# A fused two-layer transformer kernel in f32: the layer norm moves from VectorE to ScalarE, several steps move by a slot or two, and in even slots the gated products run between the two bias steps

## The reference

```
xn = layernorm(x)
x  = x + attn0(xn) + ffn0(xn)      # 16 heads, rope, window bias, causal softmax,
                                   # relu(probs + tau/row), Wo; FP4-quantised silu-gated FFN, I = 352
xn = layernorm(x)
x  = x + attn1(xn) + moe1(xn)      # linear attention: elu(q)+1, elu(k)+1, running state;
                                   # 4 experts (top 2) and a shared one, I = 344
layernorm(x) = (x - mean) / sqrt(var + 1e-5)
```

## Time and profile before

| what | value |
|---|---|
| median of three runs | 2307.14 us |
| profiled execution | 2310.34 us |
| its span on the core | 2308.5 us |
| mean granted TensorE clock | 0.971 of full speed |
| busy: TensorE / its weight loads | 2078.7 / 1355.0 us |
| busy: VectorE / ScalarE / GpSimd | 1635.0 / 1400.3 / 1147.4 us |
| instructions | 52509 |

### The profile page before, as it was taken

The page is one execution under the profiler, slowest core; times in us unless marked ns, Lnnn a source line. Parts: engine busy times, 40 slices in busy tenths (PEclk is TensorE's granted clock), DMA queues, the critical chain, the costliest instruction groups (busy, mean ns, idle before and its releaser), DMA issues.

```text
span 2308.5 us, 52509 instructions
## 1 busy us (share of the span) xinstructions
PE 2078.7 (90%) x18761; PEld 1355.0 (59%) x18761; DVE 1635.0 (71%) x5384; ACT 1400.3 (61%) x3797; POOL 1147.4 (50%) x1800
## 2 busy tenths in 40 slices
PE   3888989989899998989989899998989999898988
PEld 1455655656566574655656566574655656566565
DVE  7557767677777767767677776767767677766756
ACT  1667566665756657566665756657566575756642
POOL 5675463745536454463645636454463745535220
PEclk7779999999999999999999999999999999999999
DMA  4000000000000000000000000000000000000000
GB/s 119 6 6 2 1 15 1 15 2 11 6 2 15 1 15 2 1 15 2 15 2 7 10 2 15 2 15 2 1 15 2 15 2 11 1 2 11 2 10 6
DMA packets 33542, 22.03 MB, mean 10 GB/s; under 512 B 2443, under 2 KB 32771, under 8 KB 33283
## 3 DMA queue, kind: packets, MB, share of 16 engines
q1 hardware_dynamic: 33283, 18.68, 2.8%
HBM read 14.48 MB, written 4.19 MB: 8 GB/s over the span
## 4 chain that ended last, share of the span: by engine, by line
PE 60%; DVE 16%; ACT 13%; issue 8%; POOL 4%; DVEq 0%; ACTq 0%; POOLq 0%
PE ps L1097 9%; PE ps L1168 9%; PE ps L1178 7%; PE ps L1237 7%; PE ps L1111 6%; ACT ring L921 4%; PE ps L1087 3%; PE ps L1066 3%; DVE ring L538 3%; ACT pb L930 3%; PE ps L1075 2%; PE ps L1222 2%; PE ps L1144 2%; PE ps L1195 2%; PE ps L1207 2%
## 5 line engine op out<-in xcount | busy, mean ns | idle before, releaser
L814 POOL TENSOR_SCALAR ring<-ring,row_rcp,tau_row 128x128 f32<-128x128 f32 (+3 forms) x1024 | 626.1, 618 | 824.4 <-DVE row_rcp L545 824.2
L921 ACT ACTIVATE ring<-ring,neg_max 128x128 f32<-128x128 f32 (+3 forms) x1024 | 572.2, 560 | 625.6 <-DVE neg_max L538 622.3
L1097 PE MATMUL ps<-identf,ring 128*128 128x128 f32 x2560 | 384.9, 288 | 17.9 <-ACT qkT L912 11.3
L930 ACT ACTIVATE pb<-ps 128x512 f32<-128x512 f32 x640 | 349.1, 585 | 23.9 <-PE ps L1097 16.8
L538 DVE CUSTOM_DVE_ANT_1 ring<-ps,bias_t 128x384 f32<-128x384 f32 (+1 forms) x496 | 287.2, 615 | 82.3 <-PE ps L1087 78.3
L1097 PEld LDWEIGHTS ps<-identf,ring 128*128 128x128 f32 x2560 | 280.1, 144 | 103.8 <-issue 62.6
L1168 PE MATMUL ps<-xn1T,eg_t 128*128 128x512 f32 (+1 forms) x480 | 265.1, 635 | 37.2 <-DVE h L592 36.9
L1237 PEld LDWEIGHTS ps<-ed_t,h 128*128 128x128 f32 (+1 forms) x1920 | 250.7, 191 | 74.7 <-issue 73.1
L1237 PE MATMUL ps<-ed_t,h 128*128 128x128 f32 (+1 forms) x1920 | 272.3, 278 | 0.0
L1178 PE MATMUL ps<-xn1T,eu_t 128*128 128x512 f32 (+1 forms) x480 | 259.3, 622 | 0.4 <-DVE h L599 0.4
L944 ACT ACTIVATE tanh_t<-ps 128x512 f32<-128x512 f32 (+2 forms) x304 | 171.9, 565 | 123.0 <-PE ps L1168 118.3
(11 more groups left out here) (161 smaller groups left out, 3208.2 us busy)
## 6 DMA issues: line engine op xcount, KB each, us to landing
x_t<-x SPq DMA_DIRECT2D x16, 256.0 KB, 2.8
x<-x SPq DMA_DIRECT2D x16, 256.0 KB, 2.8
out<-x SPq DMA_DIRECT2D x16, 256.0 KB, 2.3
bias_t<-bias SPq DMA_DIRECT2D x1, 1536.0 KB, 7.7
eg_t<-eg SPq DMA_DIRECT2D x1, 860.0 KB
eu_t<-eu SPq DMA_DIRECT2D x1, 860.0 KB
ed_t<-ed SPq DMA_DIRECT2D x2, 320.0 KB
ring<-inv_row SPq DMA_DIRECT2D x1, 256.0 KB, 2.7
```

The source lines that it names most:

```text
L814: pool.tensor_scalar(e, e, row_rcp[:, m % 2, r:r + 1], tau_row[:, i, HG * g + r:HG * g + r + 1], ALU.mult, ALU.add).then_inc(p_ok.sem, 1)
L921: act.activation(e, e, ACT.Exp, bias=neg_max[:, n % 2, r:r + 1], scale=-1.0, accum_out=row_sum[:, n % 2, r:r + 1]).then_inc(exp_ok.sem, 1)
L930: act.activation(pb[:, c % NPB, :], bank(turn_bank(q)), ACT.Relu).then_inc(t_taken[q % 2].sem, 1)
L1097: last = pe.transpose(o[:, r * P:(r + 1) * P], ring_of(i, r)[:, k * P:(k + 1) * P], idf)
```

## The change

- `norm` leaves VectorE. There `norm_shift` computes -mean x rstd for the four tiles (one 128x4 instruction), and ScalarE computes Identity(x rstd + shift) in four activations, each with a scale and a bias pointer, in slot 2 (layer 0) and slot 17 (layer 1). ScalarE takes over the wait on the turn of xq.
- `fp4_steps` of x moves from slot 3 to 4, the steps after it (VectorE `fp4_magic` 6 to 7; GpSimd 4, 7, 8, 9 to 5, 8, 9, 10) by one slot each. The turn stays in slot 11.
- `elu_m` gets a third buffer; `elu_high`, `stack_high` and `stack_low` of layer 1 come one slot later.
- `blocks_before`: PV of steps with i = 0 comes four slots back instead of two.
- `STACK0` 27, 59 become 26, 58. `HID_AMAX` 15, 17, 19, 21 become 18, 19, 34, 35.
- In even slots `products` moves from behind `biased(s + 1)` and the extras to between `biased(s)` and `biased(s + 1)`.

```diff
-STACK0 = (27, 45, 59, 69)
-HID_AMAX, HID_STEP, HID_SCALED = [p + 3 for p in GATE0], 36, (38, 39, 40, 41)
+STACK0 = (26, 45, 58, 69)
+HID_AMAX, HID_STEP, HID_SCALED = (18, 19, 34, 35), 36, (38, 39, 40, 41)
...
     def blocks_before(self, f, s):
-        return self.blocks(*divmod(SLOTS * f + s - 2, SLOTS))
+        near, far = (self.blocks(*divmod(SLOTS * f + s - back, SLOTS)) for back in (2, 4))
+        return [blk for blk in far if STEPS[blk[1]][1] == 0] + [blk for blk in near if STEPS[blk[1]][1]]
...
+        shift = sb("shift", [P, 2, T])
...
-        elu_m = sb("elu_m", [P, 2, 2 * D])
+        elu_m = sb("elu_m", [P, 3, 2 * D])
...
+        shift_ok = two("norm_shift_ready")
...
-            def norm(b, layer, src, dst):
+            def norm_shift(b, layer):
-                for t in range(T):
-                    dve.tensor_scalar(dst[:, t, :], src[:, t, :], moments[:, layer, t, 0:1], rstd[:, layer, t:t + 1],
-                                      ALU.subtract, ALU.mult).then_inc(xn_ok[layer].sem, 1)
+                dve.scalar_tensor_tensor(out=shift[:, layer, :], in0=moments[:, layer, :, 0], scalar=-1.0, in1=rstd[:, layer, :],
+                                         op0=ALU.mult, op1=ALU.mult).then_inc(shift_ok[layer].sem, 1)
...
             def elu_low(b, t):
-                if t >= 2:
-                    dve.wait_ge(elu_ok.sem, elu_ok.at(b, t - 1))
-                dve.tensor_scalar(elu_m[:, t % 2, :], qk[:, t, :], 0.0, None, ALU.min).then_inc(elum_ok.sem, 1)
+                if t >= 3:
+                    dve.wait_ge(elu_ok.sem, elu_ok.at(b, t - 2))
+                dve.tensor_scalar(elu_m[:, t % 3, :], qk[:, t, :], 0.0, None, ALU.min).then_inc(elum_ok.sem, 1)
             def elu_high(b, t):
-                dve.scalar_tensor_tensor(out=qk[:, t, :], in0=qk[:, t, :], scalar=0.0, in1=elu_m[:, t % 2, :],
+                dve.scalar_tensor_tensor(out=qk[:, t, :], in0=qk[:, t, :], scalar=0.0, in1=elu_m[:, t % 3, :],
...
                 if p == 2:
-                    norm(b, 0, x_t, xn)
+                    norm_shift(b, 0)
...
                 if p == ADD_X1 + 3:
-                    if has(b + 2):
-                        dve.wait_ge(t_ps.sem, plan.turn["xq", b + 2, 0] + 1)
-                    norm(b, 1, x1, xn1)
+                    norm_shift(b, 1)
-                if 0 <= p - QKV1 - 4 < T:
-                    elu_high(b, p - QKV1 - 4)
+                if 0 <= p - QKV1 - 5 < T:
+                    elu_high(b, p - QKV1 - 5)
...
-                if p == 3:
+                if p == 4:
                     dve.wait_ge(xn_ok[0].sem, xn_ok[0].at(b, T))
...
-                if p == 6:
+                if p == 7:
                     dve.wait_ge(x_scaled.sem, x_scaled.at(b, 1))
...
                 if has(f) and s % 2 == 0:
                     biased(f, s)
+                if s % 2 == 0:
+                    for b, p in plan.beside(f, s):
+                        products(b, p)
+                if has(f) and s % 2 == 0:
                     biased(f, s + 1)
                 for b, p in plan.beside(f, s):
                     for name, k in at(EXTRAS, p):
                         from_scores(b, name, k)
-                for b, p in plan.beside(f, s):
-                    products(b, p)
+                if s % 2:
+                    for b, p in plan.beside(f, s):
+                        products(b, p)
...
-                if p == 4:
+                if p == 5:
                     pool.wait_ge(x_step_ok.sem, x_step_ok.at(b, 3))
...
-                if p == 7:
+                if p == 8:
                     pool.wait_ge(x_magic.sem, x_magic.at(b, 2))
...
-                if p == 8:
+                if p == 9:
                     pool.wait_ge(x_fp4.sem, x_fp4.at(b, 1))
...
-                if p == 9:
+                if p == 10:
                     pool.wait_ge(x_fp4.sem, x_fp4.at(b, 2))
...
-                if 0 <= p - QKV1 - 6 < T:
-                    stack_low(b, 1, p - QKV1 - 6)
+                if 0 <= p - QKV1 - 7 < T:
+                    stack_low(b, 1, p - QKV1 - 7)
...
             def elu_exp(b, t):
-                act.activation(elu_m[:, t % 2, :], elu_m[:, t % 2, :], ACT.Exp).then_inc(elue_ok.sem, 1)
+                act.activation(elu_m[:, t % 3, :], elu_m[:, t % 3, :], ACT.Exp).then_inc(elue_ok.sem, 1)
+
+            def norm(b, layer, src, dst):
+                act.wait_ge(shift_ok[layer].sem, shift_ok[layer].at(b, 1))
+                for t in range(T):
+                    act.activation(dst[:, t, :], src[:, t, :], ACT.Identity, bias=shift[:, layer, t:t + 1],
+                                   scale=rstd[:, layer, t:t + 1]).then_inc(xn_ok[layer].sem, 1)
             def beside(b, p):
+                if p == 2:
+                    norm(b, 0, x_t, xn)
+                if p == ADD_X1 + 3:
+                    if has(b + 2):
+                        act.wait_ge(t_ps.sem, plan.turn["xq", b + 2, 0] + 1)
+                    norm(b, 1, x1, xn1)
...
-                if 0 <= p - QKV1 - 5 < T:
-                    stack_high(b, 1, p - QKV1 - 5)
+                if 0 <= p - QKV1 - 6 < T:
+                    stack_high(b, 1, p - QKV1 - 6)
```

## The result

The changed kernel takes 2266.95 us in the median of four runs (2263.96 to 2269.08), the kernel before 2305.94 in four runs beside it (2302.63 to 2309.8): ratio 0.9829, 95% interval 0.9809 to 0.985. That is 39 us less, inside the range given and in the direction given, but 2.5 times the 15.5 us of the sum.

A forecast was written before the change was run, and what follows sets the result against it. TensorE's own work was taken as the floor, with at most 11 us idle per pass. Gains of 0.2 + 0.55 + 0.4 - 0.05 = 1.1 us over 14.5 passes, less 0.5 for the drain, gave 2291.6 us, range 2262 to 2309.

The forecast's parts named there:

- one pass stands for all: Whole kernel: the program repeats 64 slots per x block, so one 137.4 us pass was read for every pass.
- the turn of the pass: Slot 62 to slot 5: 0.6 gained at slots 4 and 5, 0.4 lost at slot 4, net gain 0.2 us a pass.
- slots 14 to 21: Layer-1 norm, hidden products and moved hidden_amax: gain 0.55 us a pass in the sum.
- tanh 2 is fixed by Exp and two probs copies: net 0.0: Slot 16: hidden 1 comes 0.2 earlier, but gate 3 then waits for tanh 2 (1015.19), so nothing is gained.
- Slots 26 to 33: Slots 26 to 32 in the sum: slot 28 starts 1.2 earlier, ScalarE can't follow, 0.4 us a pass stays.
- Slots 42 to 49: Slots 46 to 48 in the sum: gate wait shrinks 0.6, but the later qkT copy delays slot 48; 0.05 us lost.
- Products between the biases: Slots 14, 26, 42, 46, 62: second Exp starts one product later, 0.52 to 0.61; effects entered slot by slot.
- ScalarE becomes the bound: Rival, chance 0.17: uncovered second Exps in slots 14, 26, 42, 46, 62 cost 0.61 each; 2321, mild form 2309.
- Start and drain: First and last passes partial, 14.5 full ones counted; drain after the last scores about 0.5 dearer from an unhurried norm.
- The waits fall in full: Rival, chance 0.22: ScalarE keeps up and waits at slots 4, 5, 14 to 21, 26, 46 go, 3.6 a pass: 2255.
- Table reloads: Rival, chance 0.02: Identity in another table, so 32 norms bring 64 loads, 82 us of ScalarE: 2345.
- The port rule: Rival, chance 0.03: GpSimd's chain after row_rcp shortens 0.3 per blocked scaling, cancelling slot 4's 0.6 wait: 2283.

The follow-up runs named there:

- Experiment 1: Kernel before with the layer-1 up product of slot 26 issued twice into the same bank, filling TensorE's wait: 2302.09 us, ratio 0.9974.
- b_fp4: Kernel before with only the FP4 steps of x one slot later, norm still on VectorE: 2282.35 us, ratio 0.9896.
- experiments 2 and 3: Before with norm on ScalarE and FP4 later 2280.81, FP4 later alone 2282.35; after with norm back on VectorE 2267.4, FP4 back in slot 3 2280.19.
- b_pv_stack: Kernel before with only PV of i = 0 two slots later and the layer-0 stacks in slots 26 and 58: 2293.3 us, ratio 0.9931.
- b_amax: Kernel before with only hidden_amax moved to slots 18, 19, 34 and 35: 2300.0 us, ratio 0.9966.
- b_norm_scalar: Kernel before with only the layer norm on ScalarE and the FP4 steps of x one slot later: 2280.81 us, ratio 0.989.
- b_between: Kernel before with only the gated products put between the two biases in even slots: 2316.09 us, ratio 1.0051.
- experiment 6: Kernel before with only hidden_amax moved to slots 18, 19, 34 and 35 (the run b_amax): 2300.0 us, ratio 0.9966.
- a_again: Kernel after run once more without any edit, to count clock drops: 2266.81 us in one execution.
- a_norm_vector: Kernel after with the layer norm back on VectorE, other edits kept, FP4 steps still a slot later: 2267.4 us, ratio 0.9839.
- experiment 2: Norm's engine: kernel before with norm on ScalarE and FP4 steps later, 2280.81 us; kernel after with norm back on VectorE, 2267.4 us.

## Why the prediction had the direction right and the size wrong

**Two steps failed: the price of the waits in the sum of a pass, and "one pass stands for all".** Of the 23.5 us that the sum missed, about 16 are clean passes (14.5 x 2.2 = 31.9 where the sum has 16.0). The two terms most undersized are the turn of the pass (0.2 in the sum, 0.69 measured) and slots 14 to 21 (0.55, measured 1.05). The rest, 7 to 8, is what is left for the clock, for which the sum has no term. That the measured time lay in the range at all owes to its lower end, which was worked out from a rival; the stretch that the forecast itself stood for was 2283 to 2302.5.

- *No term for the clock.* The pass from which all was read, frame 7, happens to be one at full clock; the next one has two drops. The page's mean clock of 0.971 was in the table and I did not ask where it was lost. That passes of 137.4 and 140.3 us stood side by side (the frame starts say it) was taken as spread. The excess over clean passes is 13.6, 9.3 and 11.7 us in three profiles of before, most of it drops, and none and 1.5 us in two of the kernel after. Experiment 1 has a clean pass of the same length and an excess of 2.1.
- *A wait was priced at its listed idle time.* In slot 4 the two waits that went are listed with 0.28 and 0.31 us, and the sum has 0.6. Alone, b_fp4 gains 1.03. TensorE in slot 4, from the timeline of b_fp4:

```profile
971.00 0.83 PE L1237 MATMUL ps<-ed_t,h 128*128 128x128 f32 x6
971.67 0.73 PE L1121 MATMUL ps<-suffix_t,xn 128*128 128x3 f32 x6
972.26 0.38 PE L1075 MATMUL ps<-ident,qx 128*128 128x128 f16 x4
```

and of the kernel before:

```profile
986.44 0.83 PE L1237 MATMUL ps<-ed_t,h 128*128 128x128 f32 x6
987.55 0.80 PE L1121 MATMUL ps<-suffix_t,xn 128*128 128x3 f32 x6 [0.28 <-DVE neg_max L538]
988.67 0.38 PE L1075 MATMUL ps<-ident,qx 128*128 128x128 f16 x4 [0.31 <-ACT pb L930]
```

From start to start the first step takes 0.67 instead of 1.11, the second 0.59 instead of 1.12: 0.44 and 0.53 gained for 0.28 and 0.31 listed. Matmuls that follow each other overlap (six take 0.83 in the row, but the next begins 0.67 after the first); behind a wait the first has no neighbour to overlap. So each wait cost 0.16 to 0.22 more than its row says.
- *Turn of the pass* (forecast 0.2): measured 0.69, 0.84 of it in slot 4. The mechanism held, and so did its counterweight: GpSimd's chain behind row_rcp starts 0.5 later in the slot (0.4 was forecast), and the wait on it goes from 0.2 to 0.7 instead of 0.6. I credited the gain to the norm leaving VectorE; experiments 2 and 3 show that the order of fp4_steps and the biases does it with the norm on either engine.
- *Slots 10 to 13*: the sum has no term, 0.20 was gained by PV two slots later (b_pv_stack has it too). "PV late: zero" looked only at its buffers, not at the wait on the pb copies that it moves away from.
- *Slots 14 to 21* (forecast 0.55): measured 1.05. b_amax gives 0.41 of it, b_norm_scalar 0.35, b_pv_stack 0.14, b_between 0.05. The norm's price was right: Identity with two pointers was put at 489 ns and four at 1.65. Groups of the kernel after by line and shape:

```profile
L958 ACT ACTIVATE xq<-x,shift,rstd 128x128 f32<-128x128 f32 x64 | 26.4, 482 | 19.6 <-DVE shift L499 19.6
L958 ACT ACTIVATE xn<-x_t,shift,rstd 128x128 f32<-128x128 f32 x64 | 26.2, 481 | 2.3 <-DVE shift L499 2.3
...
L958 ACT ACT_TABLE_LOAD x1 | 1.3, 1283 | 8.1 <-DVE shift L499 8.1
```

and its place, in time order on ScalarE and TensorE of the kernel after the earlier trace rows:

```profile
993.40 1.65 ACT L958 ACTIVATE xq<-x,shift,rstd 128x128 f32<-128x128 f32 x4 [0.76 <-DVE shift L499]
```

```profile
995.10 0.66 PE L1071 MATMUL ps<-identf,xq 128*128 128x128 f32 x4 [0.99 <-ACT xq L958]
995.60 0.76 PE L1191 MATMUL ps<-wuq,xnT 128*128 128x352 f32 x2
```

Slot 18 starts at 991.69 here and at 1014.91 before. The turn of xn1 comes 0.5 later in the slot (0.2 was forecast), up 3 right behind it 0.3 earlier (0.4 was forecast): the fork was read right. What failed is "tanh 2 is fixed by Exp and two probs copies: net 0.0". Exp itself waits for VectorE's bias behind hidden_amax, and with the reduction gone the whole row of ScalarE up to tanh 2 comes 0.35 earlier (experiment 6).
- *Slots 26 to 33* (forecast 0.4): measured 0.55 in slots 26 to 30. The 0.18 more in slot 34 is the longer of its two lengths (0.01 in a_again). "ScalarE can't follow" is what happened: the gate wait at slot 27 is gone, slot 26 is 1.64 shorter and slot 28 0.95 longer. ScalarE works 11.64 of 12.01 us there, and ScalarE's timeline of the kernel after has the qkT copy end at 1018.90, 13.1 us after slot 26 began, 0.5 sooner than before (forecast: 0.4):

```profile
1017.89 1.01 ACT L917 COPY qkT<-ps 128x1024 f16<-128x1024 f16 x1
```

- *Slots 42 to 49* (forecast 0.05 lost): measured 0.13 lost, but elsewhere. Slot 46 is 0.62 shorter and slot 48 0.61 longer, as worked out, and cancel; the loss is in slots 42 and 44 (0.14), where the sum has no term and which b_pv_stack has too.
- *Products between the biases*: its pieces in the sum are 0.4 against it at slot 4, 0.15 for it at slot 20 and 0.05 against it at slot 48, so 0.3 a pass against it. Measured are 0.36 against it; the pieces were read about right, but they were never added up by themselves, and so the loss was not seen. The rival "ScalarE becomes the bound" fits this part and no other.
- *Start and drain.* The drain is 1.3 dearer, not 0.5. The start has a term that I left out, the first norm on ScalarE behind the table load, 2.1 us on the path by a_norm_vector; the FP4 steps a slot later give it back (first scores 2.1 earlier in b_fp4).

**The rivals.** *The waits fall in full* (2255) is nearer to the measured time than my forecast, by luck: the waits did not fall in full, but were dearer than listed, and the clock came on top. *Table reloads*: one load, as before. *The port rule*: GpSimd's chain behind row_rcp, in its timeline of the kernel after the earlier trace rows:

```profile
957.83 0.77 POOL L819 TENSOR_SCALAR ring<-ring,row_rcp,tau_row 128x512 f32<-128x512 f32 x1 [1.29 <-DVE row_rcp L547]
...
962.89 0.77 POOL L819 TENSOR_SCALAR ring<-ring,row_rcp,tau_row 128x512 f32<-128x512 f32 x1
```

takes 5.83 us where it took 5.88, and its last scaling 0.77 for 0.83: the 0.06 of one instruction, nothing more. The prediction asked only what VectorE's norm does to GpSimd; here it is the other way round (experiment 2). GpSimd had mostly begun first, and the norm ended 0.08 us behind it, so that VectorE's 2.38 us hold over 1 us of waiting and GpSimd had nothing to win back. The Trainium skill (SBUF — State Buffer, section SBUF: two separate sides) says that of a GpSimd and a VectorE instruction that both need the shared pair of ports, the one that starts first has it for its whole length and the other is blocked. The trace agrees, with 73 norms of 0.38 to 0.84 us that end behind GpSimd, and 55 of 0.33 to 0.35.

**What stays open.** What picks the passes in which the clock falls. More idle time in slot 26 goes with more drops, but b_fp4 with the full 2.07 us has none. No rule of length follows from the counts. The kernels other than before and after were profiled once each, and so was the one that fills the wait. Nor was it tried to fill the wait around the start of slot 40, which is 1.04 us (0.77 and 0.26) in all kernels and had a drop in 18 of 234 passes. Open too is what picks the two lengths of slot 34.

## What to carry to other kernels

Before a pass is taken for all, compare the lengths and the granted clock of several: a kernel whose TensorE is 90% busy can still lose 10 us to its clock behind one wait. Price a wait of TensorE at its listed idle time plus what the matmul behind it would have overlapped, and read off the trace, start to start, what that is. And try the parts of a change alone, and undone in the whole: here the plainest one, three small instructions moved behind the two that TensorE waits for, was worth 25 us alone and 13 when undone, and one part was a loss. The gains of the parts alone (25, 15, 15 and 8 us, less 12 for the loss) add up to more than the 39 of the whole; each counts drops of the clock that any one of them takes away.

## What the runs showed of the hardware

- The granted clock falls to 1.2 GHz behind a wait in a kernel that otherwise holds 2.4 GHz: in slot 26 in 28 of 117 passes of the seven kernels that leave most of the wait (1.59 to 2.07 us), in none of 117 of the eight that shorten or fill it (0.83 to 1.50), 1.1 to 1.4 us each time; in slot 40 in 18 of 234, in slots 18 and 20 in 4, always behind idle time of TensorE. With a redundant matmul in the wait the kernel took 0.26% less (0.1% by the medians).
- A VectorE instruction from SBUF to SBUF (128x128 f32, 0.33 us alone) takes up to 0.84 us when it starts while a GpSimd instruction runs, and ends 0.08 us behind it: 73 of the 128 norms of the kernel before. The profile counts it as busy time of VectorE, not as a wait.
- Six 128x128 matmuls in a row last 0.83 us, but the next begins 0.67 after the first; behind a listed wait of 0.28 and 0.31 us this overlap is lost, and removing the waits gave 0.44 and 0.53.
- The table load of 1.28 us falls on the first activation that ScalarE meets; if that one waits for data, so does the load, behind the data.
